# First tile of a gated cross-attention and expert block: unused transposes ahead of TensorE's first work, W_kv's copies on VectorE, another order of loads

## The reference

```python
x = x + tanh(g_xattn[0]) * xattn(layernorm(x), ctx)
x = x + tanh(g_ffn[0]) * ffn(layernorm(x))

def xattn(q, enc):                       # 16 heads of 16 features
    kv = (enc @ W_kv.T + b_kv).reshape(B, S, heads, d_k, 2)
    k, v = kv[..., 0], kv[..., 1]        # K and V interleaved in W_kv's rows
    scores = einsum('bshd,bstd->bsht', q, k) / sqrt(d_k)   # heads against heads of the same token
    context = einsum('bsht,bstd->bshd', softmax(scores), v)
    return context @ W_out.T + b_out

def ffn(x):                              # 8 experts, each takes its 64 best tokens of a sequence
    probs = softmax(x @ gate_w.T)
    g, m = top_k(probs.transpose(0, 2, 1), 64)
    out = zeros_like(x).at[m].add(g * (gelu(x[m] @ w1) @ w2))
```

## Time and profile before

| what | value |
|---|---|
| median of three runs | 709.1 us (707.91, 709.65, 709.1) |
| the profiled execution | 708.93 us; its span, first to last instruction, 707.0 us |
| granted TensorE clock, mean of the span | 0.974 |
| busy: PE, DVE, ACT, POOL | 655.4 (93%), 596.8 (84%), 432.2 (61%), 536.7 (76%) us |
| VectorE in tenths, first eleven of 40 slices of 17.7 us | 4, then ten times 9 |
| chain that ended last, by engine | PE 67%, DMA 9%, issue 7%, DVE 7%, POOL 5%, ACT 3% |
| HBM | 126.63 MB read, 33.55 MB written, 227 GB/s |

### The profile page before, as it was taken

The page is one execution under the profiler, slowest core; times in us unless marked ns, Lnnn a source line. Parts: engine busy times, 40 slices in busy tenths (PEclk is TensorE's granted clock), DMA queues, the critical chain, the costliest instruction groups (busy, mean ns, idle before and its releaser), DMA issues.

```text
span 707.0 us, 11529 instructions
## 1 busy us (share of the span) xinstructions
PE 655.4 (93%) x3896; PEld 536.1 (76%) x3896; DVE 596.8 (84%) x783; ACT 432.2 (61%) x1079; POOL 536.7 (76%) x498
## 2 busy tenths in 40 slices
PE   5799999973799999999999999989999999999996
PEld 2456556533688888877888888868888899999995
DVE  4999999889999999999899999998999351676763
ACT  4677677662777777876677777856766633233321
POOL 2889989997868888988888889898888625435343
PEclk9999999975899999999999999999999999999999
DMA  5777688562548777777887777768877868999992
GB/s 154 246 246 235 204 281 256 188 214 81 171 157 238 239 238 238 224 236 201 241 247 241 239 239 223 224 207 232 230 227 228 270 178 268 323 313 300 320 275 34
DMA packets 97072, 160.96 MB, mean 228 GB/s; under 512 B 8171, under 2 KB 74486, under 8 KB 97014
## 3 DMA queue, kind: packets, MB, share of 16 engines
q1 hardware_dynamic: 84150, 142.91, 60.4%
q0 software_dynamic: 12288, 16.79, 13.1%
q10 hardware_dynamic: 576, 0.52, 0.2%
HBM read 126.63 MB, written 33.55 MB: 227 GB/s over the span
## 4 chain that ended last, share of the span: by engine, by line
PE 67%; DMA 9%; issue 7%; DVE 7%; POOL 5%; ACT 3%; POOLq 0%; SPq 0%; DVEq 0%
PE bank L1103 20%; PE bank L1086 19%; DMA out_dram<-ys,ids 8%; PE bank L1015 6%; PE bank L1035 4%; PE bank L1130 4%; PE bank L987 3%; PE bank L1120 3%; DVE prod_v L475 2%; PE bank L1074 2%; DVE co L477 1%; PE bank L1047 1%; PE bank L1018 1%; POOL prod_p L330 1%; POOL out_dram L398 1%
## 5 line engine op out<-in xcount | busy, mean ns | idle before, releaser
L1086 PE MATMUL bank<-xin,w1in 128*128 128x256 f32 x1536 | 204.5, 290 | 8.8 <-DVE xin L642 5.4
L1086 PEld LDWEIGHTS bank<-xin,w1in 128*128 128x128 f32 x1536 | 193.4, 196 | 10.3 <-issue 9.8
L1103 PE MATMUL bank<-w2s,hT 128*128 128x256 f32 x768 | 175.4, 382 | 0.0
L398 POOL DMA_INDIRECT out_dram<-ys,ids x64 | 104.5, 1633 | 75.9 <-ACT ys L824 57.7
L1103 PEld LDWEIGHTS bank<-w2s,hT 128*128 128x128 f32 x768 | 142.4, 190 | 17.7
L810 ACT ACTIVATE hT<-bank 128x512 f32<-128x512 f32 x128 | 76.2, 598 | 112.2 <-PE bank L1086 100.1
L477 DVE TENSOR_REDUCE co<-prod_v 128x208 f32<-128x3328 f32 (+2 forms) x32 | 109.7, 3428 | 1.1
L475 DVE TENSOR_TENSOR prod_v<-bank,Ex 128x3328 f32<-128x3328 f32 (+2 forms) x32 | 109.6, 3423 | 0.1
L330 POOL TENSOR_TENSOR prod_p<-kvs,q 128x1024 f32<-128x1024 f32 (+2 forms) x32 | 89.7, 2802 | 15.8 <-ACT q L778 10.4
L384 POOL DMA_INDIRECT xg<-xn_scratch,ids x64 | 65.4, 1021 | 32.2 <-issue 16.7
L338 POOL TENSOR_TENSOR tree_a<-prod_p 128x512 f32<-128x512 f32 (+2 forms) x64 | 85.9, 1342 | 4.7
(11 more groups left out here) (143 smaller groups left out, 1120.3 us busy)
## 6 DMA issues: line engine op xcount, KB each, us to landing
w1in<-w_parts SPq DMA_DIRECT2D x128, 512.0 KB
w2s<-in_L_ffn_w_dram SPq DMA_DIRECT2D x32, 1024.0 KB
w_parts<-w1s SPq DMA_DIRECT2D x32, 512.0 KB, 3.2
w1raw<-in_L_ffn_w_dram SPq DMA_DIRECT2D x32, 256.0 KB, 4.4
ct<-in_ctx_dram SPq DMA_DIRECT2D x32, 128.0 KB
xt<-in_x_dram SPq DMA_DIRECT2D x32, 128.0 KB
out_dram<-x SPq DMA_DIRECT2D x32, 128.0 KB
xn_scratch<-xn SPq DMA_DIRECT2D x32, 128.0 KB
```

The lines of the kernel that those rows point to most:

```text
L398: pool.indirect_dma_start(out=out_rows[:, :], out_offset=bass.IndirectOffsetOnAxis(ap=ids[:, g % 2, p * E + e:p * E + e + 1], axis=0), in_ ...
L1086: ins = pe.matmul(HB[k % 2][:, D * f:D * (f + 1)], w1in[:, k, w, c, P * f:P * (f + 1)].bitcast(f32r), xin[:, n % 2, x_, c, :], start=(m == ...
L1103: ins = pe.matmul(dst, hT[:, n % 2, f, cols], w2s[:, n % 2, f, :], start=(f == 0), stop=(f == FC - 1))
```

## The change

The unused transposes write the bank XT, which nothing reads at that time. `setup_ev` is split into `wkvT_ready` and `rest_ready`, `out_bias_scaled` is new. The scaling of b_out moves from VectorE to ScalarE, the load of x of tile 0 from SyncE's queue to ScalarE's.

```diff
@@ SyncE
             sp.dma_start(bias_row[0:1, 2 * D:3 * D], b_out.rearrange("(o n) -> o n", o=1)).then_inc(setup_b, 16)
+            load_c(0)
             sp.dma_start(gates[:, 0:1], g_xattn.rearrange("(a n) -> a n", a=1).broadcast_to([P, 1])).then_inc(gates_loaded, 16)
             sp.dma_start(gates[:, 1:2], g_ffn.rearrange("(a n) -> a n", a=1).broadcast_to([P, 1])).then_inc(gates_loaded, 16)
-            load_c(0)
-            load_x(0)
@@ VectorE
+            def take_wkvT(c):
+                dve.wait_ge(setup_t, c + 1)
+                src = bank[4 + 2 * c]
+                dve.tensor_copy(wkvT[:, c, 0:D], src[:, 0:D]).then_inc(wkvT_ready, 1)
+                dve.tensor_copy(wkvT[:, c, D:2 * D].rearrange("p (d t) -> p t d", t=H),
+                                src[:, D:2 * D].rearrange("p (t d) -> p t d", d=DK)).then_inc(wkvT_ready, 1)
+
             for i, cols in enumerate((slice(0, 2 * D), slice(2 * D, 3 * D))):
                 if i == 1:
-                    dve.wait_ge(gates_tanh, 1)
-                    dve.tensor_scalar(bias_row[0:1, cols], bias_row[0:1, cols], tanh_g[0:1, 0:1], None, ALU.mult).then_inc(bias_rows, 1)
-                    dve.wait_ge(bias_rows, 3)
+                    for c in range(DC):
+                        take_wkvT(c)
+                    dve.wait_ge(out_bias_scaled, 1)
@@ ScalarE
+            act.dma_start(xt[:, 0, :], x_t[0]).then_inc(x_loaded[0], 16)
+            act.wait_ge(eps_ready, 1)
+            act.activation(exp_warm[:, :], eps[:, :], ACT.Exp)
+            take_ctT(0)
             act.wait_ge(gates_loaded, 2 * 16)
             act.activation(tanh_g[:, :], gates[:, :], ACT.Tanh).then_inc(gates_tanh, 1)
-            act.wait_ge(eps_ready, 1)
+            act.wait_ge(setup_b, 3 * 16)
+            act.wait_ge(gates_tanh, 1)
+            act.activation(bias_row[0:1, 2 * D:3 * D], bias_row[0:1, 2 * D:3 * D], ACT.Copy, scale=tanh_g[0:1, 0:1]).then_inc(out_bias_scaled, 1)
             act.wait_ge(ve_set, 1)
             x_stats(0)
-            take_ctT(0)
-            for c in range(DC):
-                act.wait_ge(setup_t, c + 1)
-                src = bank[4 + 2 * c]
-                act.activation(wkvT[:, c, 0:D], src[:, 0:D], ACT.Copy)
-                act.activation(wkvT[:, c, D:2 * D].rearrange("p (d t) -> p t d", t=H),
-                               src[:, D:2 * D].rearrange("p (t d) -> p t d", d=DK), ACT.Copy).then_inc(setup_ev, 1)
             make_q(0)
@@ TensorE
-                        pe.wait_ge(setup_ev, c + 1)
+                        pe.wait_ge(wkvT_ready, 2 * c + 2)
...
+            def warm_up(n):
+                for _ in range(n):
+                    pe.transpose(XT[:, 0:P], ident[:, :], ident[:, :])
+
             pe.wait_ge(ident_ready, 2)
+            warm_up(22)
             ctx_transposes(0)
+            warm_up(3)
             pe.wait_ge(setup_loaded, 4 * 16)
...
-            pe.wait_ge(setup_ev, 2 * DC)
+            pe.wait_ge(rest_ready, DC)
```

More of the change, by code:

```diff
@@ L175, in flamingo_gated_block_kernel @@
         ident_ready, consts_ready, base_ready = sem("ident_ready"), sem("consts_ready"), sem("base_ready")
-        setup_t, setup_ev = sem("setup_t"), sem("setup_ev")
+        out_bias_scaled = sem("out_bias_scaled")
+        setup_t, wkvT_ready, rest_ready = sem("setup_t"), sem("wkvT_ready"), sem("rest_ready")
         bias_rows, bias_step, bias_moved = sem("bias_rows"), sem("bias_step"), sem("bias_moved")
@@ L858, in _ @@
                 act.activation(woT[:, c, :], src[:, 0:D], ACT.Copy, scale=tanh_g[:, 0:1])
-                act.activation(gwT[:, c, :], src[:, D:D + E], ACT.Copy).then_inc(setup_ev, 1)
+                act.activation(gwT[:, c, :], src[:, D:D + E], ACT.Copy).then_inc(rest_ready, 1)
             take_ctT(1)
```

## The result

The changed kernel takes 705.9 us (median of five runs, 704.82 to 706.69) against 709.08 (707.91 to 709.65): ratio 0.9958, 95% interval 0.9941 to 0.9975. A second measurement of both gave 706.22 (ten runs) against 708.32 (fourteen): 0.9971, 0.9959 to 0.9983. The profiled execution's span is 704.4 us (707.0 before), its own time 706.44.

A forecast was written before the change was run, and what follows sets the result against it. The prediction took one string of waits at the start, with TensorE at its lower clock level, as the bound: 708.93 - 3.4 + 0.3 = 705.8, carried to the median, 706.0 us; own range 704.8 to 707.0, whole range 704.2 to 709.0.

The forecast's parts named there:

- The view it rested on: Up to 15.15 us one string of waits without a second branch; what comes off the start is passed on to the end.
- Step 2: TensorE's warm-up: unused transposes raise the clock between 5 and 7 us; W_kv's transposes start at 6.8 and end near 7.9.
- Step 3: W_kv's copies on VectorE: 0.42 us each, from 7.4 to 9.1; the first projection's four products end near 10.3.
- Step 4: ScalarE's string becomes the last: x_stats(0) at about 7.5, q at 11.05; tile 0 starts 3.4 us earlier (2.8 to 3.9).
- Step 5: SyncE's queue: loads behind the bias go out 1.9 to 2.1 us later; tile 0's exponentials give back 0.3 us.
- loads bind: Rival, chance 0.08: bias_step at 12 instead of 10.9, exponentials at 21.6; a gain of 1.9, 707.2 us.
- a sign of being wrong: A granted clock below 1 where it was 1.00 before, above all in the blocks that follow routing.
- The sum: Whole kernel: 708.93 - 3.4 + 0.3 = 705.8 us, carried to the median as 706.0.
- The forecast's own range: 704.8 to 707.0 us, from terms 3.9 and 2.8 and half a block of clock either way.
- The no-rise rival: Unused transposes at the start don't raise TensorE's clock: 0.5 us earlier than before, 708.6 us as a median; chance 0.25.
- The slower rival: TensorE's clock is lost once more further on, in two more blocks and a projection: loss 6.4, 712.4 us; chance 0.12.

The follow-up runs named there:

- e1: The kernel before with only the 22 + 3 unused transposes added: 706.38 us against 708.44, ratio 0.9968.
- e9: e5 with x of tile 0 loaded ahead of W_kv, x_stats(0) ahead of take_ctT(0) and 16 + 3 unused transposes: 705.56 us against 708.32, ratio 0.9959.
- e6: The changed kernel with the edits of e4 and e5 together: 705.05 us against 708.63, ratio 0.9956.
- e4: The changed kernel with x_stats(0) ahead of the tanh and the scaling of b_out on ScalarE: one run, 705.57 us.
- the second profile: The changed kernel profiled once more, unedited: ahead of before by 2.46 us at tiles 0 to 9 and 2.76 at the last tile.
- the second profile of before: The kernel before profiled once more, unedited: -0.25, +0.55 and +0.58 us from its first profile at tiles 0 to 9, tile 15 and the last.
- e7: The changed kernel with W_kv's four copies back on ScalarE, between x_stats(0) and make_q(0): 707.71 us against 708.44, ratio 0.9992.
- e5: The changed kernel with x and c of tile 2, x of tile 3 and four slices of w1 loaded ahead of SyncE's wait: one run, 705.81 us.
- e3: The changed kernel with the two gates issued ahead of the context of tile 0 again: one run, 706.18 us.
- e2: The changed kernel without the unused transposes: 706.81 us against 708.44, ratio 0.9978.

## Why the prediction was right

Time and range held (706.0 forecast, 705.9 measured), and the mechanism is in the main the forecast one. That the times agree to 0.1 us is luck: the second measurement gave a gain of 2.1 us (1.2 to 2.9 by its interval) where 3.1 was forecast. The two intervals share 1.8 to 2.9, and the leads at the last tile, 2.57 and 2.76, lie in it, so 3.1 was probably somewhat high. Step by step:

- *The view it rested on*, that the start is one string and what comes off it is passed on whole: shown. The lead is 2.92 to 2.96 us at each of the first ten tiles. But the change has three parts, and the prediction priced them as one; by e1 the transposes alone bring what all three do.
- *Step 2, the clock.* Right that unused transposes raise it, which I gave 0.55 against 0.25. From 1.55 us on TensorE did nothing but transposes, and it came to the upper level at about 5 us in e9 (two transposes in 0.39), at about 7 in the changed kernel (0.63 for the context's two, then 1.04 for W_kv's eight). The forecast of a rise at 5 to 7 was at its late end here, which put W_kv's transposes at 7.16 instead of 6.8, and in e6 it was past it. The Trainium skill's rule ("TensorE: Matmul & The Clock Gate", Part 4: transpose-mode doesn't count as PE-busy in the same way) is contradicted by these rows for 128x128 float32 transposes as far as it says that the full clock doesn't engage; whether they count less than full products stays open, though the one profile with full products showed no earlier rise.
- *Step 3.* The plain copies take 0.42 us as taken, the strided ones 0.58, near the upper bound of 0.60. They end at 9.5, forecast 9.1; the products at 10.85, forecast 10.3. Hidden, as said, behind q at 11.67.
- *Step 4, mis-sized by 0.4 us.* Right that ScalarE's string sets tile 0 in the changed kernel's first profile. The tanh did not "wait about as long": it came at 7.40, since the gates landed at 7.4 and the context's copy, held by the unused transposes, ended then as well; the scaling took 0.51, not 0.4. So x_stats(0) started at 8.12 instead of 7.5. From there to q it was 3.55 us, exactly as summed, and kvs ended 0.48 us behind q instead of 0.65. Tile 0 came 2.99 us earlier, forecast 3.4. The landing of x was put too early as well (6.9 to 7.4; x_stats(0) waited for it until 7.72 in e4), but the tanh hid this.
- *Step 5, about right in kind, its price not met.* bias_b went out at 11.20, forecast 10.9. The exponentials came at 20.58, forecast 20.4 to 20.5, but two errors meet there: the scores themselves were ready only at 20.55, not at 20.1, and the queue was hidden. In the second profile the queue did end last, with 0.75 us given back by `con`, forecast 0.3. In e4, where bias_b went out at 12.02 as in the rival "loads bind", the loss was 0.7 us where the rival had 1.5 (21.6 for 20.1), and it came through x of tile 2 and q of tile 1, which by the prediction had tenths "to spare", not through the slice.
- *Left out: TensorE's clock at tile 1.* A granted clock below 1 in stretches where it was 1.00 was named as a sign of being wrong, and there is one, 13.8 to 20.6. It cost 0.06 us, the whole of what tile 0 gave back in the first profile, and was covered by the queue in the second.
- *The sum*, 3.1 us, met 2.92 and 2.46 at tile 0 and 2.57 and 2.76 at the last tile. Its two errors (3.4 for 2.99, 0.3 for 0.06) partly cancelled. The forecast's own range doesn't follow from its terms: 3.9 and 2.8, with half of 2.34 either way, give 704.4 to 707.8, not 704.8 to 707.0.
- *The no-rise rival's time* (708.6) is not tested: without the transposes TensorE isn't held up either, and that kernel was at 706.8.
- *The slower rival* named the right unknown with the wrong size: low stretches moved in every profile, and the lead of the changed kernel grew by 0.53 and 1.25 us from tile 9 to 15 and shrank by 0.9 at tiles 22 to 24 in its two profiles; it never lost 6.4. In the four profiles of the two kernels, behind 184 us, a block of 24 products that met a low stretch took 4.33 to 4.61 us instead of 3.1, and only in the second profile of before 5.46: mostly 1.2 to 1.5 us each and not the 2.34 of the prediction.

## What to carry to other kernels

Look for cold TensorE work on the one string that everything waits for; filling its idle time with unused transposes is cheap, but the filling stands ahead of the real work too, so end it when the data has landed, and keep idle spells between it and the work it is meant for short: behind 1.4 us of it the products ran at the lower level in e7 (3.68 us instead of 1.98), though not in e9. Test each part of a change alone: here the transposes alone brought as much as the whole can be told to bring, and the rest without them most of it. Before moving an operation, list what is queued behind its semaphore on other engines: here the load queue behind a bias split gave back up to 0.75 us. When a change moves a few microseconds, compare the same mark tile by tile: it separates what the change did from where the clock happened to fall.

## What was unexpected of the hardware

The granted clock in the records reads 1.00 from the start in the kernel before, while the durations are those of the lower level until 14.3 us; it first reads below 1.00 after a fall.

The length of one idle spell of TensorE doesn't tell whether the clock falls. Spells of 1.42 us stood ahead of falls in e7 (9.03 to 10.45, fall at 10.5) and in the changed kernel (12.12 to 13.54, fall at 13.8), and one of 0.77 us ahead of a fall at 14.5 in e6. Spells of 1.40 us in e9, 1.51 in e5 and 1.82 in e4 had no fall behind them: the products that followed took 1.98 or 1.99 us.

The two gates, loads of 128 elements of 4 bytes each, landed 2.8 to 4.8 us after their issue in the profiles of both kernels. TensorE's wait for a 128 KB load queued behind them (the context of tile 0) ended 4.1 to 4.8 us after its issue (both profiles of before, e3), its wait for one queued ahead of them 3.0 us after (e2).
